# Attention over 3202 keys: the last two keys taken out of the tile loop

## The chip, the cores and the metric

The kernel runs on one core of a Trainium2 chip. The metric is the device time of one execution in microseconds (us): 2633.38 as the median of 3 runs, 2632.97 to 2635.46. All inputs and outputs are float32.

## The reference

One block: a cross attention with a residual, then a mixture of two out of eight experts with a residual. The change touches the attention alone.

```
q = (layernorm(x) @ Wq + bq)     # 4096 x 512, 16 heads of 32
k = (ctx @ Wk + bk)              # 3202 x 512
v = (ctx @ Wv + bv)
A = softmax(q k^T / sqrt(32))    # per head: 4096 queries x 3202 keys
x = x + (A v) @ Wo + bo
x = x + experts(layernorm(x))    # router, top 2 of 8
```

3202 keys are 25 tiles of 128 and two keys over.

## The kernel before

The program has three stages: the projections (about 0 to 292 us), the attention (to about 2142 us), then the output projection, the router and the experts. `attention` (L754) is the stage of interest.

It works in 32 iterations: 4 groups of 4 heads (`NG`), and for each group 8 chunks of 512 queries (`NC`). One iteration runs over `NT` = 26 tiles of 128 keys. The last tile holds `LAST` = 2 keys and is padded: `k_st` is filled to 3328 columns and `v_st` with a zeroed 26th tile.

For a tile, TensorE first makes the scores (`scores`, L1104 to L1130): keys are the stationary operand, 97 rows deep (three rounded parts of 32 rows, and one row that subtracts a shift), and 512 queries stream. The output has keys on partitions. A *pair* is two heads, so it fills two PSUM banks; a tile has two pairs, and `NP` = 52 pairs make an iteration. Three slots of two banks (`S_RING` = 3) hold pairs, so pair n waits until pair n-3 has been exponentiated. ScalarE turns a pair into probabilities with one Exp over 1024 columns (L1020) and writes them to `probs`, a ring of 6 tiles with three more places for the last three tiles. It waits for the earlier user of a place: TensorE's product with the values, and VectorE's addition. TensorE multiplies probabilities with values (`weigh`, L1144, helper `over_keys`, L1137 to L1142): four heads side by side in four column groups of the array, as eight float32 instructions, into bank 6.

The softmax's denominators take a second way. VectorE adds the tiles of probabilities elementwise into `sums[b]` (`add`, L1053 to L1068), 128 x 2048 at a time; two buffers `sums` alternate by iteration. The tiles named in `SUM_ON_PE`, here 13 and 25, are left out there: TensorE multiplies them with `ones` into bank 7. That leaves 24 tiles and 23 additions on VectorE. Early in the next iteration (`SUMS_AT`, behind tile 2's values) `sum_up` multiplies `sums` with `ones` into the same bank and so closes the denominators. ScalarE copies them out (L986, before pair 14), GpSimd's queue spreads them over partitions by DMA, VectorE inverts them (L745, behind addition 9), GpSimd's queue broadcasts the inverses, VectorE multiplies (L751, `normalise`, behind addition 13), ScalarE rounds the result (L992) and GpSimd subtracts for the low part (L867).

The order on each engine is written out by hand. TensorE's is set by `burst_end` (L1132): before it weighs tile t it issues scores up to pair 2t + 7, rounded up so that bursts end where a ring of three slots ends. As 52 is not a multiple of 3, the slots and burst ends shift by one from iteration to iteration and repeat every three.

The keys and values of a group are reloaded in three pieces on SyncE's queue as the previous group's last iteration leaves them (`keys`, `values`). In iteration 0 SyncE also loads `Wo` into `sums[1]` (L949), and ScalarE waits for it before pair 17 and rounds it (L1008).

Of the kernel before, what the change touches and what calls it, by code (L numbers as in the profile page):

```python
# [54 lines left out]
SUM_ON_PE = (13, 25)  # L55
SUMS_AT = 2
SUMS_COPY_AT, INVERT_AT, NORMALISE_AT, SPLIT_AT = 14, 9, 13, 36
# [696 lines left out]
def attention(nc, mem, sb0, sem, psum, unbounded, g):  # L754
# [3 lines left out]
    NP = 2 * NT  # L758
    ROWS = 3 * DH
    FILLS = 3  # L760
# [6 lines left out]
    with mem:  # L767
# [3 lines left out]
        k_st = sb("k_st", [SH + 1, HG, SP_], F32R)  # L771
        q_st = sb("q_st", [SH + 1, 2, HG, CH], F32R)
        v_st = sb("v_st", [P, NT, P], F32)
        ones = sb("ones", [P, DH], F32)
        probs = sb("probs", [P, P_RING + LAG, HG, CH], F32)
# [13 lines left out]
        rows_filled = [sem(f"rows_filled{n}") for n in range(K_PIECES)]  # L789
# [16 lines left out]
        pe_added = sem("pe_added")  # L806
# [18 lines left out]
        def s_slot(phase, n):  # L825


            return (phase * NP + n) % S_RING

# [15 lines left out]
        def fill_rows(eng, heads):  # L845

            for n, (a, m) in enumerate(pieces):
                eng.memset(k_st[SH:SH + 1, heads[0]:heads[1], a * P:min((a + m) * P, S)].bitcast(F32), 1.0).then_inc(rows_filled[n], 1)

        with nc.Block() as block:  # L850
            @block.gpsimd
            def _(pool):
                fill_rows(pool, (0, HG // 2))

                for n in range(K_PIECES):
                    pool.wait_ge(rows_filled[n], 2)
# [12 lines left out]
                def divide(it):  # L869
                    spread_sums(pool, results, it)  # L870
                    broadcast_inverses(pool, results, it)
                    low(it)

                for it in range(NIT - 1):
                    divide(it)

            @block.sync
            def _(sp):
# [21 lines left out]
                def keys(j, before, n):  # L900
                    a, m = pieces[n]
                    if before is not None:

                        sp.wait_ge(s_ready, before * NP + 2 * (a + m))
                    load_k(sp, j, a * P, min((a + m) * P, S) - a * P, k_in[n])

                def values(j, before, n):
                    a, m = pieces[n]
                    if before is not None:

                        sp.wait_ge(pv_done, before * NT + (a + m))
                    full = m - (n == K_PIECES - 1)
                    sp.dma_start(v_st[:, a:a + full, :], v_d[:, a:a + full, ds(j * P, P)]).then_inc(v_in[n], 16)
                    if n == K_PIECES - 1:
                        if before is None:

                            sp.wait_ge(filled, FILLS)
                        sp.dma_start(v_st[0:LAST, NT - 1, :], v_d[0:LAST, NT - 1, ds(j * P, P)]).then_inc(v_in[n], 16)
# [29 lines left out]

                sp.dma_start(wo_raw[:], g["Wo"].rearrange("(j p) n -> p j n", p=P)).then_inc(wo_in, 16)  # L949
# [22 lines left out]
            def _(act):  # L972
# [21 lines left out]
                def step(it, phase):  # L994
                    first = isinstance(it, int) and it == 0
                    for n in range(NP):
# [6 lines left out]
                        t, half = divmod(n, 2)  # L1003
                        slot = s_slot(phase, n)
                        if first and n == NP // 3:

                            act.wait_ge(wo_in, 16)
                            act.activation(wo_hi, wo_raw[:], ACT.Copy).then_inc(wo_hi_ready, 1)  # L1008

                        act.wait_ge(s_ready, it * NP + (n + 1))  # L1010
                        if half == 0:

                            ago, u = before(t)
                            if not (first and ago):
                                act.wait_ge(pv_done, (it + ago) * NT + (u + 1))
                                if u in add_of:
                                    act.wait_ge(added, (it + ago) * adds + add_of[u])
                                if u in SUM_ON_PE:
                                    act.wait_ge(pe_added, (it + ago) * len(SUM_ON_PE) + SUM_ON_PE.index(u) + 1)
# [3 lines left out]
                for it in range(NIT):  # L1023
                    step(it, it % S_RING)
# [3 lines left out]
            def _(dve):  # L1028

                dve.memset(k_st[:, :, S:SP_].bitcast(F32), 0.0).then_inc(filled, 1)  # L1030
                dve.memset(v_st[:, NT - 1, :], 0.0).then_inc(filled, 1)
                dve.memset(ones[:], 1.0).then_inc(filled, 1)
                fill_rows(dve, (HG // 2, HG))
# [21 lines left out]

                def add(it, b, k):
                    t = on_dve[k + 1]

                    dve.wait_ge(exp_done, it * NP + (2 * t + 2))
# [10 lines left out]
                def step(it, b):  # L1070
                    for k in range(adds):
                        add(it, b, k)
# [14 lines left out]
            def _(pe):  # L1087
# [23 lines left out]
                def scores(it, u, i_of, n, first):  # L1111

                    b, (t, half) = u % 2, divmod(n, 2)
# [3 lines left out]
                    if t in piece_of and half == 0:  # L1117

                        pe.wait_ge(k_in[piece_of[t]], (i_of // (NC // 2) + 1) * 48)
                        if first:  # L1120
                            pe.wait_ge(rows_filled[piece_of[t]], 2)
                    slot = s_slot(u % S_RING, n)
# [10 lines left out]
                def burst_end(u, t):  # L1133

                    e = 2 * t + LEAD
                    return e + (S_RING - 1 - e - u) % S_RING
# [7 lines left out]
                def weigh(it, i, t):  # L1144
                    if t in piece_of:

                        n = piece_of[t]
                        pe.wait_ge(v_in[n], (i // (NC // 2) + 1) * (16 * (1 + (n == K_PIECES - 1))))

                    pe.wait_ge(exp_done, it * NP + (2 * t + 2))  # L1150
# [7 lines left out]
                    if t in SUM_ON_PE:  # L1158
                        n = LAST if t == NT - 1 else P
                        if t == SUM_ON_PE[0]:  # L1160

                            pe.wait_ge(sums_copied, it)
                        over_keys(SUM_BANK, lambda h: ones[0:n], lambda h: probs[0:n, p, h, :], t == SUM_ON_PE[0],
                                  False).then_inc(pe_added, 1)
# [8 lines left out]
                def step(it, u, i, i_next):  # L1173

                    first = isinstance(it, int) and it == 0
                    n = 0 if first else burst_end(u - 1, NT - 1) + 1 - NP
                    for t in range(NT):
                        while n <= burst_end(u, t):
# [4 lines left out]
                            n += 1  # L1183
                        weigh(it, i, t)
# [703 lines left out]
```

## Time and profile before

| | |
|---|---|
| median of 3 runs | 2633.38 us |
| the profiled execution's own time | 2634.78 us |
| its span, first to last instruction | 2633.0 us |
| PE busy | 2504.0 us, 95% |
| DVE (VectorE) busy | 2190.0 us, 83% |
| ACT (ScalarE) busy | 1879.6 us, 71% |
| POOL (GpSimd) busy | 487.6 us, 19% |
| granted TensorE clock | 0.971 of full speed, mean |

The shares are means over three stages with different limits. A matmul's end is modelled, so a busy PE isn't a PE at its peak: overlapping matmuls have a duration longer than the distance of their starts, and the distance is what counts. The same holds for a chain of instructions on one engine: the work of an engine is read from starts, not from durations.

### The profile page before, as it was taken

The numbers are of one execution on the slowest core, as the hardware profiler recorded it, in microseconds if no ns is written. First come the engines' busy times: TensorE is split into PE (matmuls) and PEld (weight loads), VectorE is DVE, ScalarE is ACT, GpSimd is POOL, SyncE is SP. The second block draws the span as 40 slices with busy tenths as digits, with TensorE's granted clock in tenths as the row PEclk, the third lists the DMA queues.
The fourth block names the chain that finished last, engine by engine and source line by source line (L and its number), as shares of the span: only waits on it lengthen the run. The fifth ranks groups of instructions, "written<-read, shape, count | busy, mean of one in ns | idle before, by whom it ended". The sixth has DMA issues, their size and how long they took to land. (4 is left out here: it accounts for less than half of the span.)

```text
span 2633.0 us, 38495 instructions
## 1 busy us (share of the span) xinstructions
PE 2504.0 (95%) x14123; PEld 1317.2 (50%) x14123; DVE 2190.0 (83%) x1810; ACT 1879.6 (71%) x2173; POOL 487.6 (19%) x548
## 2 busy tenths in 40 slices
PE   8999489999999999999999999999999988979998
PEld 7878234444434444444444444444444447768776
DVE  4378479999999999999999999999999965666555
ACT  3123379888888888888988889888888855613333
POOL 2123101110000111000011001011000034325664
PEclk9999789999999999999999999999999999969999
DMA  7445861111142111115111111511111038724463
GB/s 260 164 140 208 180 174 26 29 27 31 38 88 63 25 29 33 36 27 113 37 29 33 34 29 25 125 30 33 25 37 25 13 122 297 247 78 135 131 215 124
DMA packets 132882, 231.61 MB, mean 88 GB/s; under 512 B 23634, under 2 KB 56922, under 8 KB 131940
## 3 DMA queue, kind: packets, MB, share of 16 engines
q1 hardware_dynamic: 110468, 177.57, 23.9%
q0 software_dynamic: 22240, 51.68, 6.5%
q8 instruction: 114, 1.87, 0.3%
q14 instruction: 60, 0.49, 0.1%
HBM read 155.32 MB, written 91.66 MB: 94 GB/s over the span
## 5 line engine op out<-in xcount | busy, mean ns | idle before, releaser
L1068 DVE TENSOR_TENSOR sums<-sums,probs 128x2048 f32<-128x2048 f32 x704 | 1644.6, 2336 | 89.9 <-ACT probs L1020 24.7
L1020 ACT ACTIVATE probs<-psum 128x1024 f32<-128x1024 f32 x1664 | 1565.2, 1039 | 207.9 <-PE psum L1129 204.9
L1129 PE MATMUL psum<-q_st,k_st 97*128 97x512 f32 x3328 | 968.6, 421 | 51.7 <-DMA q_st<-shift_scratch 23.1
L1129 PEld LDWEIGHTS psum<-q_st,k_st 97*128 97x128 f32 x3328 | 565.4, 189 | 679.3 <-ACT probs L1020 535.8
L1141 PE MATMUL psum<-probs,v_st 128*32 128x512 f32 x6656 | 835.8, 601 | 0.0
L1141 PEld LDWEIGHTS psum<-probs,v_st 128*32 128x32 f32 x6656 | 158.5, 108 | 370.5 <-issue 300.0
L1836 PE MATMUL psum<-we_hi,wo 128*128 x624 | 219.6, 413 | 8.3 <-issue 5.7
L730 POOL DMA_DIRECT2D sum_scratch<-shared_rows x32 | 18.9, 591 | 989.7 <-ACT shared_rows L986 989.3
L1689 ACT ACTIVATE wo<-psum 128x512 fp32r<-128x512 f32 x78 | 46.5, 597 | 135.6 <-PE psum L1822 112.0
L1836 PEld LDWEIGHTS psum<-we_hi,wo 128*128 128x128 f32 x624 | 119.7, 192 | 35.1 <-issue 9.4
L1836 PE MATMUL psum<-we_lo,wo 128*128 x312 | 124.7, 400 | 0.0
L1682 ACT ACTIVATE shared_rows<-hold 128x512 f32<-128x512 f32 x78 | 63.2, 811 | 65.3 <-DMA hold<-token_rows,near 36.6
L338 POOL TENSOR_TENSOR squares<-o_hi 128x512 fp32r<-128x512 f32 (+1 forms) x60 | 60.6, 1018 | 207.2 <-ACT o_hi L376 120.1
L867 POOL TENSOR_TENSOR shared_rows<-shared_rows 128x512 fp32r<-128x512 f32 x31 | 58.6, 1890 | 217.5 <-ACT shared_rows L992 217.5
L1513 PE MATMUL psum<-wo,att_hi 128*128 128x512 f32 x256 | 85.3, 415 | 7.4 <-DMA att_lo<-ol_scratch 7.4
L1068 DVE TENSOR_TENSOR sums<-probs 128x2048 f32<-128x2048 f32 x32 | 73.2, 2288 | 14.3 <-ACT probs L1020 14.2
L1746 DVE TENSOR_TENSOR res<-psum,be_all 128x512 f32<-128x512 f32 x52 | 36.0, 691 | 56.8 <-PE psum L1836 54.6
L376 ACT ACTIVATE o_hi<-psum,bk_col 128x512 fp32r<-128x512 f32 (+1 forms) x28 | 17.4, 640 | 91.6 <-PE psum L591 91.6
L740 POOL DMA_DIRECT2D shared_rows<-inv_scratch x128 | 63.5, 502 | 49.8 <-DMA inv_scratch<-spread_inv 49.8
L737 POOL DMA_DIRECT2D inv_scratch<-spread_inv x32 | 17.5, 548 | 287.3 <-DVE spread_inv L745 273.9
L1141 PE MATMUL psum<-probs,ones 2*32 2x512 f32 (+1 forms) x512 | 67.3, 596 | 0.0
L1836 PEld LDWEIGHTS psum<-we_lo,wo 128*128 128x128 f32 x312 | 60.2, 193 | 11.2
(197 smaller groups left out, 2036.6 us busy)
## 6 DMA issues: line engine op xcount, KB each, us to landing
q_st<-qh_scratch SPq DMA_DIRECT2D x64, 256.0 KB
token_rows<-rows SPq DMA_DIRECT2D x8, 1040.0 KB, 5.2
xn<-in_x SPq DMA_DIRECT2D x16, 512.0 KB, 6.7
qh_scratch<-o_hi SPq DMA_DIRECT2D x8, 1024.0 KB, 4.5
ql_scratch<-o_lo SPq DMA_DIRECT2D x8, 1024.0 KB, 7.8
q_st<-ql_scratch SPq DMA_DIRECT2D x32, 256.0 KB
token_rows<-in_x SPq DMA_DIRECT2D x1, 8192.0 KB, 33.6
shared_rows<-inv_scratch POOLq DMA_DIRECT2D x128, 64.0 KB, 2.2
```

The source lines that it names most:

```text
L338: pool.tensor_tensor(squares[:, j, 0:w], h, h, ALU.mult).then_inc(squared, 1)
L740: pool.dma_start(a["recip"][h * DH:(h + 1) * DH, :], a["inv_d"][h:h + 1, :].to_broadcast([DH, CH])).then_inc(a["inv_in"], 16)
L867: pool.tensor_tensor(o_low, o_sb, o_high.bitcast(F32), ALU.subtract).then_inc(low_ready, 1)
L1020: nc.scalar.activation(probs[:, p_slot[t], 2 * half:2 * half + 2, :], psum[:, 2 * slot:2 * slot + 2, :], ACT.Exp, scale=SCALE).then_inc(ex ...
L1068: nc.vector.tensor_tensor(sums[b][:], a[:], probs[:, p_slot[t]], ALU.add).then_inc(added, 1)
L1129: mm = nc.tensor.matmul(psum[:, 2 * slot + h % 2, :], k_st[:, h, t * P:(t + 1) * P], q_st[:, b, h, :], start=True, stop=True)
L1141: mm = nc.tensor.matmul(psum[h * DH:(h + 1) * DH, bank, :], lhs(h), rhs(h), start=start, stop=stop)
L1513: mm = pe.matmul(psum[:, i % WO_BANKS, :], A[b][:, j, r, :], W[:, j, :], start=t == 0, stop=t == len(terms) - 1)
L1682: act.activation(xs[s % 2], r[:, 0:D], ACT.Identity, bias=r[:, SHIFT_AT:SHIFT_AT + 1], scale=r[:, RSTD_AT:RSTD_AT + 1]).then_inc(xs_done, 1)
L1689: act.activation(x_hi[s % 2], psum[:, T_BANK + s % 2, :].rearrange("p (k n) -> p k n", k=KT), ACT.Copy).then_inc(xh_done, 1)
L1746: dve.tensor_tensor(res[s % RES][:, 0:D], psum[:, OUT_BANKS[s % 4], :], be_all[:, ds(e, 1), :].rearrange("p o n -> p (o n)"), ALU.add).the ...
L1836: mm = pe.matmul(psum[:, OUT_BANKS[s % 4], :], A[s % 2][:, k, :], W[:, k, ds(e, 1), :].rearrange("p o n -> p (o n)"), start=t == 0, stop=t ...
```

## The change

The tile of two keys goes. `NT` becomes 25 and `NP` 51. The two keys of all four heads, eight rows, become one extra pair, number `REST_PAIR` = 36, that takes one slot of the ring but only its first bank:

- TensorE multiplies, for each of the four heads, a stationary operand of 97 x 72 with the head's queries, and accumulates all four in one bank. Of the 72 rows of output 0 to 7, 32 to 39 and 64 to 71 hold the same eight rows of scores. The operands are columns of `rest_k`, which is zero elsewhere.
- ScalarE takes Exp of 72 x 512 into `rest_probs`; two pairs later it rounds that into `rest_split`.
- VectorE, ahead of addition 19, replaces rows 32 to 39 of `rest_split` by the rounding's remainder.
- TensorE, ahead of tile 22's values, multiplies `rest_v` and `rest_ones` with `rest_split`, into banks 6 and 7, one instruction each (`weigh_rest`).

VectorE copies the two keys' columns of `k_st` to three places of `rest_k` once per group of heads, ahead of addition 9 of its first iteration. `rest_v` is made once, in iteration 0, from twelve small loads on SyncE's queue that come ahead of the load of `Wo`.

`SUM_ON_PE` is tile 12 alone, so VectorE has 24 tiles and 23 additions as before. The places of the steps at the iteration's start move by one tile or one addition. As 51 is a multiple of 3, all iterations have the same slots and burst ends. A ring place whose sum is on PE is released by the next tile's `pv_done` in place of a semaphore of its own.

The diff, cut to its core:

```diff
-SUM_ON_PE = (13, 25)
-SUMS_AT = 2
-SUMS_COPY_AT, INVERT_AT, NORMALISE_AT, SPLIT_AT = 14, 9, 13, 36
+SUM_ON_PE = (12,)
+SUMS_AT = 3
+REST_PAIR = 36
+REST_AT = 22
+REST_KEYS_AT = 9
+REST_LOW_AT = 19
+SUMS_COPY_AT, INVERT_AT, NORMALISE_AT, SPLIT_AT = 16, 10, 14, 38
...
-    NP = 2 * NT
+    NT = NT - 1
+    REST = HG * LAST
+    REST_ROWS = 2 * DH + REST
+    NP = 2 * NT + 1
...
+                sp.wait_ge(filled, FILLS)
+                for o in (0, DH, 2 * DH):
+                    for h in range(HG):
+                        sp.dma_start(rest_raw[o + h * LAST:o + (h + 1) * LAST, :, h * DH:(h + 1) * DH],
+                                     v_d[0:LAST, NT, :].rearrange("p (j x) -> p j x", j=NG)[:, :, h * DH:(h + 1) * DH]).then_inc(wo_in, 16)
                 sp.dma_start(wo_raw[:], g["Wo"].rearrange("(j p) n -> p j n", p=P)).then_inc(wo_in, 16)
...
-                            act.wait_ge(wo_in, 16)
+                            act.wait_ge(wo_in, 16 * (3 * HG + 1))
                             act.activation(wo_hi, wo_raw[:], ACT.Copy).then_inc(wo_hi_ready, 1)
+                            act.wait_ge(rest_v_stage, 3)
+                            act.activation(rest_v[:], rest_raw[:], ACT.Copy).then_inc(rest_v_stage, 1)
+                        if n == REST_PAIR + 2:
+                            act.wait_ge(exp_done, it * NP + (REST_PAIR + 1))
+                            if not first:
+                                act.wait_ge(rest_used, it)
+                            act.activation(rest_split[:], rest_probs[:], ACT.Copy).then_inc(rest_high, 1)
                         act.wait_ge(s_ready, it * NP + (n + 1))
+                        if n == REST_PAIR:
+                            if not first:
+                                act.wait_ge(rest_ready, it)
+                            nc.scalar.activation(rest_probs[:], psum[0:REST_ROWS, 2 * slot, :], ACT.Exp, scale=SCALE).then_inc(exp_done, 1)
+                            continue
...
                     for k in range(adds):
+                        if k == REST_KEYS_AT and it % NC == 0:
+                            dve.wait_ge(filled, FILLS)
+                            dve.wait_ge(k_in[K_PIECES - 1], (it // NC + 1) * 48)
...
+                            for o in (0, DH, 2 * DH):
+                                dve.tensor_copy(rest_places(o), k_st[:, :, S - LAST:S])
+                        if k == REST_LOW_AT:
+                            dve.wait_ge(rest_high, it + 1)
+                            dve.tensor_tensor(rest_split[DH:DH + REST, :], rest_probs[DH:DH + REST, :],
+                                              rest_split[DH:DH + REST, :].bitcast(F32), ALU.subtract).then_inc(rest_ready, 1)
+                        if k == REST_LOW_AT and it == 0:
+                            dve.wait_ge(rest_v_stage, 4)
+                            dve.tensor_tensor(rest_v[2 * DH:], rest_raw[2 * DH:], rest_v[2 * DH:].bitcast(F32), ALU.subtract).then_inc(rest_v_stage, 1)
                         add(it, b, k)
...
+                    if n == REST_PAIR:
+                        if it % NC == 0:
+                            pe.wait_ge(added, it * adds + REST_KEYS_AT + 1)
+                        for h in range(HG):
+                            mm = nc.tensor.matmul(psum[0:REST_ROWS, 2 * slot, :], rest_k[:, h * REST_ROWS:(h + 1) * REST_ROWS],
+                                                  q_st[:, b, h, :], start=h == 0, stop=h == HG - 1)
+                        mm.then_inc(s_ready, 1)
+                        return
...
+                def weigh_rest(it):
+                    pe.wait_ge(rest_ready, it + 1)
+                    if it == 0:
+                        pe.wait_ge(rest_v_stage, 5)
+                    nc.tensor.matmul(psum[:, O_BANK, :], rest_v[:, it // NC, :], rest_split[:], start=False, stop=False)
+                    nc.tensor.matmul(psum[:, SUM_BANK, :], rest_ones[:], rest_split[:], start=False, stop=False).then_inc(rest_used, 1)
...
+                        if t == REST_AT:
+                            weigh_rest(it)
                         weigh(it, i, t)
```

## Rows read from the trace of the kernel before

**Rows 1.** Busy time by stretch: length, then each engine's busy us (instructions), clock, DMA, GB/s.

```profile
382.78:2140.34 1757.56, 1746.43 (x10422) 717.46 (x10421) 1679.30 (x776) 1556.05 (x1702) 173.46 (x248) 1.00 0.17 40
```

**Rows 2.** Timeline, VectorE alone: an iteration's first addition (start us, us, engine, line).

```profile
311.80 2.29 DVE L1068 TENSOR_TENSOR sums<-probs 128x2048 f32<-128x2048 f32 x1 [11.32 <-ACT probs L1020]
...
1007.02 2.29 DVE L1068 TENSOR_TENSOR sums<-probs 128x2048 f32<-128x2048 f32 x1
...
1064.06 2.29 DVE L1068 TENSOR_TENSOR sums<-probs 128x2048 f32<-128x2048 f32 x1 [0.26 <-ACT probs L1020]
...
1120.70 2.28 DVE L1068 TENSOR_TENSOR sums<-probs 128x2048 f32<-128x2048 f32 x1
...
1176.92 2.29 DVE L1068 TENSOR_TENSOR sums<-probs 128x2048 f32<-128x2048 f32 x1
```

**Rows 3.** Timeline of one iteration: VectorE's additions and what stands between them.

```profile
1012.28 19.07 DVE L1068 TENSOR_TENSOR sums<-sums,probs 128x2048 f32<-128x2048 f32 x8 [0.58 <-ACT probs L1020]
...
1031.26 0.24 DVE L745 RECIPROCAL spread_inv<-spread 128x16 f32<-128x16 f32 x1
1031.45 9.48 DVE L1068 TENSOR_TENSOR sums<-sums,probs 128x2048 f32<-128x2048 f32 x4
...
1040.84 0.69 DVE L751 TENSOR_TENSOR shared_rows<-shared_rows 128x512 f32<-128x512 f32 x1
...
1041.45 22.36 DVE L1068 TENSOR_TENSOR sums<-sums,probs 128x2048 f32<-128x2048 f32 x9
...
1042.65 2.23 POOL L867 TENSOR_TENSOR shared_rows<-shared_rows 128x512 fp32r<-128x512 f32 x1 [6.84 <-ACT shared_rows L992]
```

**Rows 4.** The same timeline: TensorE and ScalarE over three tiles, and the extras.

```profile
1029.48 1.65 PE L1129 MATMUL psum<-q_st,k_st 97*128 97x512 f32 x6
1030.25 5.61 ACT L1020 ACTIVATE probs<-psum 128x1024 f32<-128x1024 f32 x6 [0.59 <-PE psum L1129]
...
1031.06 1.06 PE L1141 MATMUL psum<-probs,v_st 128*32 128x512 f32 x8
...
1035.67 1.67 PE L1129 MATMUL psum<-q_st,k_st 97*128 97x512 f32 x6
...
1040.90 1.04 PE L1141 MATMUL psum<-probs,ones 128*32 128x512 f32 x8
...
1041.76 1.04 PE L1141 MATMUL psum<-probs,v_st 128*32 128x512 f32 x8
...
1066.66 1.06 PE L1141 MATMUL psum<-probs,ones 2*32 2x512 f32 x8
1066.79 0.60 ACT L980 ACTIVATE shared_rows<-psum 128x512 f32<-128x512 f32 x1 [0.94 <-PE psum L1141]
...
1067.65 1.06 PE L1141 MATMUL psum<-probs,v_st 128*32 128x512 f32 x8
```

**Rows 5.** Timeline at the attention's start: VectorE's memsets.

```profile
293.46 0.17 DVE L1031 MEMSET v_st<- 128x128 f32 x1
293.59 0.09 DVE L1032 MEMSET ones<- 128x32 f32 x1
293.78 0.27 DVE L848 MEMSET k_st<- 1x256 f32 x1
```

**Rows 6.** Timeline of iteration 0: the load of `Wo` and who waits.

```profile
323.31 0.43 SPq L949 DMA_DIRECT2D sums<-in_Wo  x1
...
338.15 1.91 ACT L1008 ACTIVATE wo<-sums 128x2048 fp32r<-128x2048 f32 x1 [13.44 <-DMA sums<-in_Wo]
...
341.00 5.92 DVE L1068 TENSOR_TENSOR sums<-sums,probs 128x2048 f32<-128x2048 f32 x1 [12.52 <-ACT probs L1020]
```

**Rows 7.** DMA of 292 to 340 us: all packets; an issue, its size, us to landing.

```profile
DMA packets 7810, 10.72 MB, mean 223 GB/s; under 512 B 1067, under 2 KB 4653, under 8 KB 7807
...
sums<-in_Wo SPq DMA_DIRECT2D x1, 1024.0 KB, 14.8
```

**Rows 8.** Timeline at the attention's end.

```profile
2140.40 1.60 PE L1141 MATMUL psum<-sums,ones 128*32 128x512 f32 x8 [1.49 <-DVE sums L1068]
```

More of the change, by code:

```diff
@@ L774, in attention @@
         ones = sb("ones", [P, DH], F32)
+        rest_k = sb("rest_k", [SH + 1, HG * (REST_ROWS + LAST)], F32R)
+        rest_v = sb("rest_v", [REST_ROWS, NG, P], F32R)
+        rest_raw = sb("rest_raw", [REST_ROWS, NG, P], F32)
+        rest_ones = sb("rest_ones", [REST_ROWS, P], F32R)
+        rest_mask = sb("rest_mask", [REST_ROWS, P], F32)
+        rest_probs = sb("rest_probs", [REST_ROWS, CH], F32)
+        rest_split = sb("rest_split", [REST_ROWS, CH], F32R)
         probs = sb("probs", [P, P_RING + LAG, HG, CH], F32)
@@ L788, in attention @@
         filled = sem("filled")
-        rows_filled = [sem(f"rows_filled{n}") for n in range(K_PIECES)]
+        rows_filled = sem("rows_filled")
+        rest_v_stage = sem("rest_v_stage")
+        rest_high = sem("rest_high")
+        rest_ready = sem("rest_ready")
+        rest_used = sem("rest_used")
         ma_k_in = sem("ma_k_in")
@@ L823, in load_q, with place, pair @@
                              src.rearrange("(h d) j l -> d h (j l)", d=DH)[:, :, ds(it * CH, CH)]).then_inc(count, 16)
-        def s_slot(phase, n):
-            return (phase * NP + n) % S_RING
+        assert NP % S_RING == 0 and LAST == 2
+        def place(t, half):
+            n = 2 * t + half
+            return n + (n >= REST_PAIR)
+        def pair(n):
+            return divmod(n - (n > REST_PAIR), 2)
         p_slot = [t % P_RING if t < NT - LAG else P_RING + t - (NT - LAG) for t in range(NT)]
@@ L843, in attention, with piece_end, fill_rows @@
         add_of = {t: max(n, 1) for n, t in enumerate(on_dve)}
-        def fill_rows(eng, heads):
+        def piece_end(n):
+            return S if n == K_PIECES - 1 else sum(pieces[n]) * P
+        def fill_rows(eng, heads, count):
             for n, (a, m) in enumerate(pieces):
-                eng.memset(k_st[SH:SH + 1, heads[0]:heads[1], a * P:min((a + m) * P, S)].bitcast(F32), 1.0).then_inc(rows_filled[n], 1)
+                eng.memset(k_st[SH:SH + 1, heads[0]:heads[1], a * P:piece_end(n)].bitcast(F32), 1.0).then_inc(count, 1)
         with nc.Block() as block:
@@ L852, in _ @@
             def _(pool):
-                fill_rows(pool, (0, HG // 2))
-                for n in range(K_PIECES):
-                    pool.wait_ge(rows_filled[n], 2)
+                fill_rows(pool, (0, HG // 2), rows_filled)
+                pool.wait_ge(rows_filled, K_PIECES)
                 pool.wait_ge(wo_hi_ready, 1)
@@ L911, in values @@
                         sp.wait_ge(pv_done, before * NT + (a + m))
[L912 to L918, printed above, removed]
+                    sp.dma_start(v_st[:, a:a + m, :], v_d[:, a:a + m, ds(j * P, P)]).then_inc(v_in[n], 16)
                 def keys_values(j, before):
@@ L1023, in _ @@
                 for it in range(NIT):
-                    step(it, it % S_RING)
+                    step(it)
                 fetch(NIT - 1)
@@ L1111, in scores @@
                 def scores(it, u, i_of, n, first):
-                    b, (t, half) = u % 2, divmod(n, 2)
+                    b, (t, half) = u % 2, pair(n)
                     if n == 0:
                         pe.wait_ge(q_in[b], (i_of + 1) * 64)
-                    if t in piece_of and half == 0:
+                    if t in piece_of and half == 0 and n != REST_PAIR:
                         pe.wait_ge(k_in[piece_of[t]], (i_of // (NC // 2) + 1) * 48)
                         if first:
-                            pe.wait_ge(rows_filled[piece_of[t]], 2)
-                    slot = s_slot(u % S_RING, n)
+                            pe.wait_ge(rows_filled, piece_of[t] + 1)
+                            pe.wait_ge(filled, FILLS + piece_of[t] + 1)
+                    slot = n % S_RING
                     if n >= S_RING:
@@ L1175, in step @@
                     first = isinstance(it, int) and it == 0
-                    n = 0 if first else burst_end(u - 1, NT - 1) + 1 - NP
+                    n = 0 if first else burst_end(NT - 1) + 1 - NP
                     for t in range(NT):
-                        while n <= burst_end(u, t):
+                        while n <= burst_end(t):
                             if n < NP:
```

53 lines of the change are left out of this document (33 added, 20 removed).

## The prediction

> **What bounds the kernel now.** I first read the busy time by stretch, to get the attention apart from the rest: from iteration 1's first addition to the last addition are 1757.56 us, at full clock, with TensorE busy 1746 us, VectorE 1679 us and ScalarE 1556 us [rows 1]. By shares TensorE would be the limit. So the next view is the timeline, by the distance of starts. It shows two engines near the limit.
>
> VectorE: the distance from one iteration's first addition to the next is 57.04, 56.64 and 56.22 us in turn [rows 2], and this triple repeats with few exceptions; over all 31 it is 1757.56 / 31 = 56.70 us. What VectorE needs, I add up from the rows of one iteration. Eight additions in a row take 19.07 us with seven waits of 0.10 us between them, so one takes (19.07 + 0.10) / 8 = 2.397 us [rows 3]. The reciprocal costs nothing: from 1012.28 to 1031.45 are 19.17 us for eight additions and the reciprocal, and eight additions alone are 19.18. An addition waits for the one before it, and a short instruction fits into that wait. `normalise` costs 0.41: from 1031.45 to 1041.45 are 10.00 us for four additions and it, against 9.59. The last nine additions take 22.36 us where nine are 9 x 2.397 - 0.10 = 21.47: 0.89 more, and GpSimd's subtraction (2.23 us) runs on SBUF just then [rows 3]. An iteration's first addition doesn't wait for its predecessor, which gives back 0.19 (the 0.10 and a start 0.08 ahead of the end, as `normalise` has it). Sum: 23 x 2.397 + 0.41 + 0.89 - 0.19 = 56.24 us. That is the shortest of the three distances, 56.22: in those iterations VectorE has no slack at all. In the others it is late by 0.42 and 0.82 us, in waits for probabilities, one of which is the 0.26 shown [rows 2] and another the 0.58 shown [rows 3].
>
> TensorE and ScalarE work as one loop: a burst of six score products, one tile of values, a burst, two tiles of values. It comes round every 1035.67 - 1029.48 = 6.19 us for three tiles [rows 4], 2.063 us each, and leaves ScalarE 0.59 us idle. For 26 tiles that is 53.6 us. On top come the ones product of the two-key tile (1067.65 - 1066.66 = 0.99), that of tile 13 (1041.76 - 1040.90 = 0.86) and `sum_up` (0.86 likewise): 56.4 us. So this pair of engines needs 56.4 and VectorE 56.2, and the mean of 56.7 is what two nearly equal limits make. A saving on TensorE alone can give back 56.70 - 56.22 = 0.48 us an iteration, 31 x 0.48 = 15 us in all. Everything added on VectorE is paid in full.
>
> **The change part by part.**
>
> *TensorE and ScalarE, per iteration.* One tile goes (2.06) and its ones product (0.99); the tile summed on TensorE stays one, `sum_up` stays. Four products of 97 x 72 with 512 columns come. A burst of six takes 1031.06 - 1029.48 = 1.58 us, 0.26 each [rows 4], so four are 1.05. The two of `weigh_rest` are 0.53 more. Sum: 56.4 - 3.05 + 1.58 = 54.9 us. ScalarE loses two Exps, inside the 2.06, and gains an Exp and a copy of 512 columns, 0.60 each by the copy of the same width [rows 4]. Beside its idle 0.59 of every three tiles they cost from nothing to 1.2 us, so the loop needs 54.9 to 56.1 us.
>
> *VectorE, per iteration.* The additions stay 23, and the reciprocal, `normalise` and GpSimd's subtraction stay, so the 56.22 stay. New is the remainder ahead of addition 19: one subtraction of 512 columns, float32 from SBUF, as `normalise` is; its eight partitions instead of 128 save nothing as far as the duration follows columns. Below, it is bounded by the reciprocal's 0.00 (16 columns) and more nearly by `normalise`'s 0.41; 0.41 is only so small because `normalise` starts 0.08 us before the addition in front of it has ended, and the next addition starts 0.08 before `normalise` ends. The new one reads and writes at partition 32, all its neighbours at partition 0. For such a step there is one row: memsets at partition 0 start 0.04 us ahead of the predecessor's end (293.46 + 0.17 against 293.59), and the one at partition 96 starts 0.10 us behind it (293.59 + 0.09 against 293.78) [rows 5]. With 0.10 on both sides the subtraction costs 0.10 + 0.69 + 0.10 - 0.10 = 0.79 us. I take 0.79, since this row is nearest in what differs, and keep 0.41 for the range. It leaves VectorE at 56.22 + 0.79 = 57.01 us, above the other loop's 56.1: VectorE becomes the only limit, and TensorE's saving is worth nothing beyond the 0.48.
>
> The Trainium skill bears on just this step. "VectorE: DVE Perf Modes", section "Two Vector instructions with no wait between them", says that an instruction which starts in another group of 32 partitions than its predecessor's input or output is held until the predecessor has finished. The memset row agrees; no subtraction in this trace crosses such a border. By the rule the step costs 0.79, and without it 0.41.
>
> *Whether VectorE is really fed.* New waits couple the engines: `weigh_rest`, ahead of tile 22's values, waits for the remainder, and behind it in TensorE's queue are tile 22 and all later scores. At that moment scores of up to the next iteration's third pair are out, so VectorE has tiles 21 to 24 to add, 4 x 2.4 = 9.6 us. TensorE then needs 0.6 for the rest, 1.0 for tile 22 and 0.8 to the first score, ScalarE 1.0: probabilities 3.4 us later. That leaves 6 us. In the other direction the reciprocal and `normalise` keep their distance of four additions, and the spreading of the sums starts two pairs later while VectorE reads it one addition later. In VectorE's queue, behind the waits for `rest_high` and `inv_in`, stand all additions; `rest_high` is made with pair 38, that is tile 18, and read ahead of the addition of tile 21. I count all of that at nothing.
>
> *The sum over iterations 1 to 31.* 31 x 57.01 = 1767.3 against 1757.6: +9.7 us. The ends are set by the last addition in both kernels: TensorE's `sum_up` has been idle for 1.49 us for it [rows 8].
>
> *Copies of the two keys.* Three small copies in four iterations. By the reciprocal's spacing (0.19) three are 0.57, of which 0.19 fit into the addition's wait: 0.4 each time, +1.5 us. Ends: 0 and 3 us. Their wait for the last piece of keys has ten additions, 24 us, since the piece was asked for.
>
> *Iteration 0.* VectorE starves there for 12.52 us because ScalarE waits 13.44 us for `Wo` [rows 6], so what is added before that point is on the path. ScalarE's rounding of `rest_v`: 0.6. The twelve small loads stand ahead of `Wo` in SyncE's queue: at 0.43 us each [rows 6] they put off its issue by 5.2. But `Wo`, 1 MB, lands 14.8 us after its issue, while 223 GB/s are moved [rows 7], which is 4.7 us for 1 MB: some 10 us are backlog, so the later issue mostly shortens the wait in it. I take 1.0, ends 0 and 5.4. VectorE adds the remainder (0.79) and, once, that of `rest_v` at partition 64 (0.79). Together +3.2 us. Memsets, mask and the fills have the 11.32 us in which VectorE waits for its first probabilities [rows 2] as cover. Outside the attention nothing changes.
>
> Total: 9.7 + 1.5 + 3.2 = +14.4 us on the span of 2633.0, on the own time 2634.8 too. That execution is 1.4 us above the median of 2633.4, so I put the difference on the median: **2647.8 us**, 0.55% slower.
>
> **The rivals.**
>
> *The remainder costs 0.41, as `normalise` does.* Then 32 x 0.38 = 12.2 and 0.4 of iteration 0 go: 2635.2 us. For it: the same form and width in the trace. Against it: the partition step of [rows 5], though that is a single row of another operation. The limit stays VectorE, at 56.63.
>
> *The remainder hides and the lateness goes: faster.* If it fitted as the reciprocal does, VectorE would need 56.22, the other loop stays below, and 31 x 0.48 = 14.9 us come back: 2633.4 - 14.9 + 1.5 + 1.6 = 2621.6 us. For it: reciprocal 0.00, and the regular burst pattern. Against it: 0.10 us of wait can't hold 0.69 us of work. It decides from a cost of 0.25 us or less.
>
> *TensorE's stop at tile 22 isn't made good.* If VectorE runs so late that each iteration TensorE's wait adds to its own 54.9 to 56.1 us, the period becomes 57.4 or so: 31 x 0.4 more, 2660 us. For it: additions run slower (2.397) than tiles come (2.063), so VectorE is always late in an iteration's second half. Against it: the 6 us above.
>
> *The twelve loads are paid in full.* 5.4 instead of 1.0: 2652 us. For it: SyncE's issues are spaced 0.43 us or more here. Against it: the backlog.
>
> **How the numbers follow.** Forecast 50% (2643 to 2652), the 0.41 rival 22% (2631 to 2638), the faster one 8%, TensorE's stop 9%, the loads 11%. The range must leave out at most the faster one and the far part of the stop's: 2631 to 2656. A measurement of this kernel tells 0.2%, 5.3 us, from no change, so slower begins at 2638.7: 50 + 9 + 11 = 70%; same is the 0.41 rival, 22%; faster 8%.
>
> **What would show it.** In the changed kernel's timeline the distance of first additions should be 57.0 us in every iteration with no wait for ScalarE; the remainder should start about 0.1 us behind an addition's end, last 0.69 and be followed at 0.1. ScalarE's idle time should now end on VectorE's additions or on TensorE waiting at `weigh_rest`. A period of 56.6 would mean the second case, 56.2 the third. Waits of additions for probabilities in steady iterations would make the whole argument wrong.

## The result: 1.2% slower, twice what was forecast

The changed kernel takes 2663.6 us (median of 4 runs) against 2633.2; ratio 1.0122, 95% interval 1.0097 to 1.0148. The forecast was 2647.8, range 2631 to 2656: right in sign, and 16 us short. The profiled execution's span is 2662.1, 29.1 above that of before.

First the timeline of the changed kernel, VectorE's first addition of an iteration, which answers to [rows 2] (start, duration):

```profile
312.74 2.29 DVE L1124 TENSOR_TENSOR sums<-probs 128x2048 f32<-128x2048 f32 x1 [10.71 <-ACT probs L1062]
...
503.04 2.29 DVE L1124 TENSOR_TENSOR sums<-probs 128x2048 f32<-128x2048 f32 x1
...
562.49 2.29 DVE L1124 TENSOR_TENSOR sums<-probs 128x2048 f32<-128x2048 f32 x1 [1.25 <-ACT probs L1062]
...
619.36 2.28 DVE L1124 TENSOR_TENSOR sums<-probs 128x2048 f32<-128x2048 f32 x1
...
676.22 2.29 DVE L1124 TENSOR_TENSOR sums<-probs 128x2048 f32<-128x2048 f32 x1
...
733.08 2.29 DVE L1124 TENSOR_TENSOR sums<-probs 128x2048 f32<-128x2048 f32 x1
...
794.42 2.29 DVE L1124 TENSOR_TENSOR sums<-probs 128x2048 f32<-128x2048 f32 x1 [4.39 <-ACT probs L1062]
```

Most iterations take 56.87 us without a wait for ScalarE: VectorE is the limit. But some are longer: 59.45 (from 503.04), 61.34 (from 733.08). Iterations are counted from 0, so 7, 15 and 23 are the last of a group; they are the turns of group. Read over all 32, the 29.1 us are:

| | us |
|---|---|
| first addition later (312.74 against 311.80) | 0.9 |
| iteration 0: 75.58 against 70.98 | 4.6 |
| iterations 1 to 31, at 56.87 each, against 1757.56 | 5.4 |
| above 56.87 at two turns of group (iterations 7 and 8, 23 and 24) | 10.9 |
| above 56.87 in iterations 1, 3, 15, 18, 20 | 8.2 |
| behind the last addition | -0.9 |

The 10.9 and the 8.2 were in no term of the forecast, but for up to 0.4 us of copies at a turn. The next rows are one undisturbed iteration of the changed kernel, at the place where ScalarE rounds the last result (compare [rows 3]):

```profile
1058.01 0.68 DVE L755 TENSOR_TENSOR shared_rows<-shared_rows 128x512 f32<-128x512 f32 x1
1058.61 10.37 DVE L1124 TENSOR_TENSOR sums<-sums,probs 128x2048 f32<-128x2048 f32 x4
1058.72 0.63 ACT L1019 ACTIVATE shared_rows<-shared_rows 128x512 fp32r<-128x512 f32 x1 [1.74 <-DVE shared_rows L755]
1059.26 0.61 ACT L1043 ACTIVATE rest_split<-rest_probs 72x512 fp32r<-72x512 f32 x1
...
1059.78 6.46 ACT L1062 ACTIVATE probs<-psum 128x1024 f32<-128x1024 f32 x7
...
1060.83 0.73 PE L1211 MATMUL psum<-q_st,k_st 97*128 97x512 f32 x2 [2.33 <-ACT probs L1062]
...
1069.01 0.68 DVE L1139 TENSOR_TENSOR rest_split<-rest_probs,rest_split 8x512 fp32r<-8x512 f32 x1
1069.72 9.48 DVE L1124 TENSOR_TENSOR sums<-sums,probs 128x2048 f32<-128x2048 f32 x4
```

ScalarE's queue is in order. It waits 1.74 us for VectorE's normalisation, all Exps wait behind it, and TensorE stands still for 2.33 us. Part of that is not the wait: the rounding (0.63) and the copy of the rest (0.61) stand in the same turn of the ring, and in a run below TensorE stops 0.50 us there though ScalarE waits for nothing. In the kernel before nothing waited there; the same rounding starts without idle time in front of it:

```profile
1041.89 0.67 ACT L992 ACTIVATE shared_rows<-shared_rows 128x512 fp32r<-128x512 f32 x1
```

VectorE has a store of tiles, so this stop alone costs nothing: that iteration takes 56.86 us. But now see the busy time by stretch of the changed kernel: the whole attention, the time before, in and behind one of the disturbances, and a turn of group (columns as in [rows 1]; the number behind POOL's is the granted clock):

```profile
388.32:2170.35 1782.03, 1719.64 (x9974) 730.45 (x9970) 1700.02 (x816) 1534.41 (x1701) 194.35 (x248) 0.98 0.17 39
503.04:541.10 38.06, 36.31 (x216) 15.50 (x215) 36.36 (x19) 31.94 (x37) 4.22 (x8) 1.00 0.03 8
541.10:551.30 10.20, 9.33 (x32) 3.14 (x32) 9.82 (x6) 6.41 (x7) 2.07 (x1) 0.50 0.21 53
551.30:562.49 11.19, 11.19 (x66) 5.40 (x66) 8.72 (x5) 9.52 (x11) 0.00 (x0) 1.00 0.31 71
...
786.90:793.70 6.80, 5.47 (x16) 2.70 (x17) 3.03 (x2) 1.36 (x2) 0.00 (x0) 0.50 1.10 221
```

The clock was 1.00 throughout the attention before [rows 1]. Now it falls to half (1.2 of 2.4 GHz) fourteen times, 78.5 us in all. Twelve of the falls begin 38 to 40 us behind an iteration's first addition, where this stop is (1060.83 - 1022.26 = 38.6). What a fall costs follows its length here: at least six of 3.4 us each cost nothing visible, those of 6.8 us in iterations 1, 18 and 20 about 1.0 us each. In iteration 3 it stays down for 10.2 us, VectorE's store runs out, and the iteration takes 2.6 us more. Iteration 15 is the third turn of group, but TensorE did not wait for keys there: it has a fall of 10.2 us like that of iteration 3, and the same 2.6 us.

And at the two other turns of group, TensorE waits for keys:

```profile
777.16 0.81 SPq L835 DMA_DIRECT2D k_st<-kh_scratch  x2
...
788.23 1.22 PE L1211 MATMUL psum<-q_st,k_st 97*128 97x512 f32 x2 [3.93 <-DMA k_st<-kl_scratch]
...
789.49 1.02 ACT L1062 ACTIVATE probs<-psum 128x1024 f32<-128x1024 f32 x1 [3.68 <-PE psum L1211]
```

SyncE asks for the next group's keys only behind the previous result's store, which waits for that same rounding. Counted from the iteration's first addition, this is at 44.1 us (777.16 - 733.08) and was at 42.1 before (764.55 - 722.46), while TensorE, a tile shorter, wants them earlier. The rows of before:

```profile
722.46 2.29 DVE L1068 TENSOR_TENSOR sums<-probs 128x2048 f32<-128x2048 f32 x1 [0.26 <-ACT probs L1020]
...
764.55 2.15 SPq L816 DMA_DIRECT2D k_st<-kh_scratch  x2
```

Behind this wait the clock falls as well (786.90 to 793.70).

### The profile page after: what moved, and what is told of

The parts are those of the page before. It is cut to its first block and busy times, and to the rows that moved or that the text cites. A ratio compares the mean times of both kernels' runs of the same rounds, so it can differ in the third digit from the quotient of the medians.

```text
span 2662.1 us, 37692 instructions
## 1 busy us (share of the span) xinstructions
PE 2484.8 (93%) x13675; PEld 1334.8 (50%) x13675; DVE 2213.9 (83%) x1859; ACT 1859.5 (70%) x2174; POOL 507.3 (19%) x548
## 5 line engine op out<-in xcount | busy, mean ns | idle before, releaser
L1062 ACT ACTIVATE probs<-psum 128x1024 f32<-128x1024 f32 x1600 | 1510.2, 1033 | 200.1 <-PE psum L1211 196.0
L1211 PE MATMUL psum<-q_st,k_st 97*128 97x512 f32 x3200 | 940.2, 426 | 102.8 <-ACT probs L1062 66.6
L1231 PE MATMUL psum<-probs,v_st 128*32 128x512 f32 x6400 | 820.7, 615 | 0.0
L895 POOL TENSOR_TENSOR shared_rows<-shared_rows 128x512 fp32r<-128x512 f32 x31 | 79.5, 2565 | 200.9 <-ACT shared_rows L1019 200.9
L1772 ACT ACTIVATE shared_rows<-hold 128x512 f32<-128x512 f32 x78 | 63.3, 811 | 63.7 <-DMA hold<-token_rows,near 36.4
L418 ACT ACTIVATE o_hi<-psum,bq_col 128x512 fp32r<-128x512 f32 x32 | 22.1, 689 | 56.4 <-PE psum L595 56.4
```

Source lines behind the costliest of these rows:

```text
L1062: nc.scalar.activation(probs[:, p_slot[t], 2 * half:2 * half + 2, :], psum[:, 2 * slot:2 * slot + 2, :], ACT.Exp, scale=SCALE).then_inc(ex ...
L1211: mm = nc.tensor.matmul(psum[:, 2 * slot + h % 2, :], k_st[:, h, t * P:(t + 1) * P], q_st[:, b, h, :], start=True, stop=True)
L1231: mm = nc.tensor.matmul(psum[h * DH:(h + 1) * DH, bank, :], lhs(h), rhs(h), start=start, stop=stop)
L1772: act.activation(xs[s % 2], r[:, 0:D], ACT.Identity, bias=r[:, SHIFT_AT:SHIFT_AT + 1], scale=r[:, RSTD_AT:RSTD_AT + 1]).then_inc(xs_done, 1)
```

## Experiments

Before each kernel's time stands its ratio to the kernel before, timed on the same chip; the absolute level differs between chips (the kernel before took 2632.8 to 2638.1 us).

**The remainder's partition.**

```diff
-   dve.tensor_tensor(rest_split[DH:DH + REST, :], rest_probs[DH:DH + REST, :], rest_split[DH:DH + REST, :] ...
+   dve.tensor_tensor(rest_split[0:REST, :], rest_probs[0:REST, :], rest_split[0:REST, :] ...
```

> The remainder is taken in rows 0 to 7 of rest_split instead of rows 32 to 39, so that the subtraction starts at partition 0 like its neighbours. In the changed kernel it costs 0.64 us (56.87 against 56.22 between first additions of undisturbed iterations). Theory A, the border between groups of partitions holds it on both sides: it costs 0.41 as the normalisation does, undisturbed iterations are 56.63 us, and 31 of them give back 7 us: about 2656. Theory B, the 0.64 is its length whatever the partition: 56.87 and 2663 stay.

Measured: 1.0110 (1.0093 to 1.0127), 2662.0 us. Undisturbed iterations take 56.62 us, so the step costs 0.40 us above 56.22, instead of 0.65. Theory A holds. The rows of this kernel show how:

```profile
998.23 10.36 DVE L1124 TENSOR_TENSOR sums<-sums,probs 128x2048 f32<-128x2048 f32 x4
1008.51 0.67 DVE L1139 TENSOR_TENSOR rest_split<-rest_probs,rest_split 8x512 fp32r<-8x512 f32 x1
1009.11 2.27 DVE L1124 TENSOR_TENSOR sums<-sums,probs 128x2048 f32<-128x2048 f32 x1
```

The remainder starts 0.08 us before the addition has ended (998.23 + 10.36) and the next addition 0.07 before its end; in the changed kernel both start 0.03 behind (1058.61 + 10.37 against 1069.01, and 1069.01 + 0.68 against 1069.72). The rule of the Trainium skill on held instructions ("VectorE: DVE Perf Modes", "Two Vector instructions with no wait between them") agrees with these starts, at 0.25 us for two borders. The total hardly moved: twelve iterations are longer than 57.5 us, six of them by 2.6, and the clock is down for 106 us.

**No remainder.** `rest_ready` is replaced by `rest_high`, and the subtraction goes.

> Leaves out the remainder of the two keys' probabilities (rows 32 to 39 then hold the rounded values a second time, so the two keys are counted twice). VectorE has 0.64 us less per iteration. Theory A (VectorE's work sets the undisturbed period, and its lateness makes ScalarE wait ahead of pair 38, TensorE stop and its clock fall): 56.22 between first additions, the waits for the normalisation shrink by up to 0.64, fewer drops of the clock within the iterations, total 2663 - 20 - some 4 = about 2639. Rival, the drops come from TensorE having less to do and not from that one stop: period 56.22 but as many drops or more, total about 2643 to 2646.

Measured: 1.0050 (1.0033 to 1.0067), 2645.6 us. 56.25 in undisturbed iterations: the need of 56.22 worked out from the rows of before was right. ScalarE's waits for the normalisation shrink too, from 34.6 us to 18.3 in all. Both fit theory A, but the total does not: A said 2639. The rival said 2643 to 2646 with as many falls or more, and there are 15 in iterations 1 to 31, where the changed kernel has 14. The falls inside groups are short (3.4 us, in iterations 0.35 us longer or not at all) but for one; the turns take 61.2, 60.9 and 62.3 us. So this run does not decide between the two. The next one does.

**ScalarE's rounding later.** `SPLIT_AT` 38 becomes 42.

> ScalarE's rounding of the last result moves from ahead of pair 38 to ahead of pair 42, so that it no longer waits for VectorE's normalisation with all Exps behind it. Theory A: the stops of TensorE at that place go, and with them the drops of the granted clock inside the groups (iterations 1, 3, 15, 18, 20 lost 8.2 us together): -8 us. But the result is stored about 3.7 us later, and the next group's keys stand behind that store in SyncE's queue: the three turns of group get longer by up to 3 us each, +5 to +9. Total 2660 to 2665, with another pattern: no drop of the clock except near 787, 1250 and 1710 us. Rival, the drops are TensorE's idle time in general: they stay where they were, total over 2668.

Measured: 1.0106 (1.0089 to 1.0123), 2660.8 us, and the pattern of theory A: iterations inside the groups lose 0.4 us in all where they lost 5.6, and the turns take 61.4, 62.6 and 61.8 (in the changed kernel 61.3, 59.5, 62.7). Around the place of the rounding three falls of 3.4 us are left, where there were twelve falls; the rival had them stay and a total over 2668. Of the 5.2 us given back inside the groups the turns took 2.2. But the edit did not do what it was made for: four pairs later ScalarE still meets VectorE, and waits for the normalisation 22 times, 30.4 us in all (34.6 in the changed kernel). What went is TensorE's stop, whose waits for ScalarE fall from 52.4 us in all to 15.9, the longest 0.85:

```profile
998.19 0.63 ACT L1019 ACTIVATE shared_rows<-shared_rows 128x512 fp32r<-128x512 f32 x1 [1.51 <-DVE shared_rows L755]
...
999.79 0.73 PE L1211 MATMUL psum<-q_st,k_st 97*128 97x512 f32 x2 [0.46 <-ACT probs L1062]
```

TensorE has the values of two tiles to work on during this wait, and the rest's copy stands four pairs away. So the place of the wait in the bursts seems to count, not its length alone.

**The same stop in the kernel before.** `SPLIT_AT` 36 becomes 32; no work is added.

> The kernel before, with ScalarE's rounding of the last result ahead of pair 32 instead of 36, so that there ScalarE has to wait some 2 to 3 us for the normalisation. Theory A: TensorE stops for 1 to 3 us per iteration at that place, the granted clock falls to half for 3 to 10 us in several iterations, and the kernel gets slower by 10 us or more, though no work is added. Rival (the stop is absorbed and the clock doesn't follow so short a stop): within 3 us of 2633, clock 1.0 throughout the attention.

Measured: 1.0642 (1.0624 to 1.0659), 2801.8 us. One constant costs 168 us. Its waits inside the attention, counted to 2140 us; it ends at 2308 (who waited for whom: total, times, longest):

```profile
ACT shared_rows L992 <- DVE shared_rows L751: 104.5, 28, 4.4
PE psum L1129 <- ACT probs L1020: 80.9, 40, 4.1
```

The clock is down for 195 us in the whole attention. Here an iteration is 3 to 7 us longer, far more than in the changed kernel. The likely reason is that TensorE's and ScalarE's loop is itself a limit in this kernel (56.4 of 56.7 us), so a stop is paid, while in the changed kernel it has slack; how the 168 us divide between stop and clock wasn't separated.

**Keys ahead of the store.** Between two groups, SyncE issues the first two pieces of keys and values ahead of the result's store, which is `late()`.

```diff
                     for n in range(K_PIECES):
+                        if n == K_PIECES - 1:
+                            late()
                         keys(j, before, n)
```

> In the last iteration of a group SyncE issues the first two pieces of the next group's keys and values ahead of the previous result's store, not behind it. In the changed kernel TensorE arrives at the next group's second tile 7 us after its keys are asked for and stops 3.9 us; the three turns of group cost 4.9, 2.6 and 6.0 us over an undisturbed period. Theory A (keys stand in SyncE's queue behind a store that waits for ScalarE's rounding): turns at iterations 7 and 23 fall to within 1 us of 56.87, the one at 15, which I put down to the clock, stays or moves; total 2663 - 9 to 12 = 2651 to 2654. Rival (the keys' transfer itself is slow there, whenever it is asked for): no change, 2663.

Measured: 1.0117 (1.0100 to 1.0134), 2667.8 beside 2638.1. The wait for keys is gone and iteration 7 takes 56.86 us: theory A on the queue. The total is a miss. The clock is now down for 109 us, every second iteration from 13 to 23 takes 59.1 to 59.5, and the gain is lost. The turns at 15 and 23 are among these (59.1 and 59.5), without a wait for keys. The stop comes in every iteration, the costly falls in some; what picks these iterations isn't shown.

**Normalisation earlier.** `INVERT_AT` 10 becomes 8, `NORMALISE_AT` 14 becomes 12.

> VectorE inverts behind addition 8 and normalises behind addition 12 (10 and 14 in the changed kernel); ScalarE's rounding stays ahead of pair 38. The normalisation then ends 4.8 us earlier, some 3 us before ScalarE asks for it. Theory A: no stop of TensorE there, no costly drop of the clock inside the groups, -8 us, and the store and the next keys some 1.7 us earlier, -2 to -4: total about 2652 to 2655. Rival (the late place of the rounding was harmless and the drops come from elsewhere): drops and total stay.

Measured: 1.0064 (1.0047 to 1.0081), 2653.8 beside 2638.1: about 15 us of the 30 are gone, a little more than expected. ScalarE still waits up to 1.3 us (16 us in all where it was 33, both counted to 2140 us). Inside the groups 1.1 us are lost where it was 5.6. In the profiled execution the attention ends 14.0 us earlier: 4.5 of it come from inside the groups, 6.2 from the turns, and 3.4 from iteration 0, which the edit hardly touches and which varies by as much between runs (next experiment).

**Small loads behind `Wo`.** The twelve loads come behind it, and ScalarE rounds `rest_v` ahead of pair 36.

> The twelve small loads of the two keys' values come behind the load of Wo on SyncE's queue, and ScalarE rounds rest_v ahead of pair 36 instead of pair 17 of iteration 0. In the changed kernel iteration 0 takes 75.58 us against 70.98, ScalarE waits 12.8 us for Wo and its rounding of rest_v delays the Exps by 0.6. Theory: both leave the path, about 2 to 3 us of the 4.6 go (the remainders' 1.3 us stay): 2660 to 2661. Rival (the extra is TensorE's and VectorE's own work in iteration 0): under 1 us.

Measured: iteration 0 takes 72.3 us where it took 75.6. But it varies: in the six runs with the loads ahead of `Wo` it took 72.2 to 75.6, mean 74.1, and in the five with them behind 71.4 to 74.1, mean 72.3. Two of these five have an addition less on VectorE. So the order is worth about 2 us, no more certain than that. The total was missed: 1.0139 (1.0122 to 1.0156), because eight iterations now take 59 us or more, with the clock down for 116 us.

**All mends in one**: partition, normalisation, keys and small loads.

> All of it in one: remainder at partition 0, normalisation earlier, keys ahead of the store, small loads behind Wo. If the 30 us are understood, every iteration from 1 on takes 56.63 us, the clock costs nothing inside the attention, iteration 0 takes 72 to 73, and the total is about 312.3 + 72.5 + 31 x 56.63 + 491 + 1.9 = 2633: no gain over the kernel before, though TensorE has 1.5 us less to do per iteration, since VectorE has 0.4 more. Over 2640 means that a part isn't understood.

Measured: 1.0018 (1.0008 to 1.0028), 2641.8 beside 2638.1. Iterations take 56.62, the longest 57.0, and the attention's last addition ends at 2141.76 us, against 2140.34 before: 28.6 of the attention's 30.0 us are back (it ended at 2170.35). The clock still falls seven times inside the attention, for 3.4 us each, without a visible cost: none of these iterations is over 56.75. The expected time was level with the kernel before, and this one is 3.7 us above it on the same chip; some 3.5 us of that lie behind the last addition (496.1 against 492.6 us to the end of the profiled executions) and stay unexplained. With one tile on TensorE no gain is left in the attention: VectorE's 56.62 stand against 56.70.

**Two tiles on TensorE**, on top of all mends; the second kernel with `SPLIT_AT` 42.

```diff
-SUM_ON_PE = (12,)
+SUM_ON_PE = (8, 17)
-REST_LOW_AT = 19
+REST_LOW_AT = 18
```

> As the run with all mends, and TensorE sums two tiles (8 and 17) in place of one, so VectorE has 22 additions; the remainder comes ahead of addition 18. VectorE then needs 56.62 - 2.40 = 54.2 us. TensorE's and ScalarE's loop was never the limit in the changed kernel, so its need isn't shown by a period; by the rows of before it is 54.9 to 56.1, plus 0.86 for the second tile: 55.8 to 57.0. If the loop needs about 56.0, iterations take 56.0 and the total is 2633 - 19 = 2614 beside 2633 of before (2618 where before is 2638). Rival, the loop needs 57: no gain, 2645. With little idle time left on TensorE the clock should not fall.

> The same with ScalarE's rounding of the last result ahead of pair 42. With two tiles off VectorE its normalisation is no longer late at pair 38, so theory A expects the same time as the run beside it within 2 us. If it is faster by over 3 us, ScalarE still waited at pair 38 with one addition less in front.

Measured: 0.9930 (0.9916 to 0.9943), 2614.8 beside 2632.8, with 56.01 us per iteration and no fall of the clock: as expected. The second, expected the same, is 0.9873 (0.9858 to 0.9888), **2600.7 us, 1.3% faster than the kernel before**, at 55.49 us. ScalarE did not wait for the normalisation in either, so that reason was wrong. With 38, its rounding stands beside the rest's copy. The rows of the first kernel, then of the second:

```profile
982.69 0.62 ACT L1021 ACTIVATE shared_rows<-shared_rows 128x512 fp32r<-128x512 f32 x1
...
983.11 1.18 PE L1216 MATMUL psum<-q_st,k_st 97*128 97x512 f32 x4
...
983.21 0.62 ACT L1048 ACTIVATE rest_split<-rest_probs 72x512 fp32r<-72x512 f32 x1
...
984.77 7.08 DVE L1129 TENSOR_TENSOR sums<-sums,probs 128x2048 f32<-128x2048 f32 x3 [1.89 <-ACT probs L1067]
...
984.79 0.73 PE L1216 MATMUL psum<-q_st,k_st 97*128 97x512 f32 x2 [0.50 <-ACT probs L1067]
```

```profile
1030.23 0.63 ACT L1048 ACTIVATE rest_split<-rest_probs 72x512 fp32r<-72x512 f32 x1
...
1030.64 1.92 PE L1216 MATMUL psum<-q_st,k_st 97*128 97x512 f32 x6
...
1031.80 7.98 DVE L1129 TENSOR_TENSOR sums<-sums,probs 128x2048 f32<-128x2048 f32 x3 [1.37 <-ACT probs L1067]
...
1034.37 0.65 ACT L1021 ACTIVATE shared_rows<-shared_rows 128x512 fp32r<-128x512 f32 x1
```

Two extra instructions in one turn of the ring stop TensorE for 0.50 us; apart, each is about what ScalarE's idle 0.59 holds. VectorE's wait shrinks by 0.52, and so does the period.

**The stop by itself**, all mends, one tile on TensorE, `SPLIT_AT` 34.

> The run with all mends (one tile on TensorE), with one constant changed: ScalarE's rounding ahead of pair 34, where it has to wait some 4 us for the normalisation. It has the undisturbed 56.62 us otherwise, so it prices the stop and the clock alone. Theory A: TensorE stops some 3 to 4 us per iteration, the granted clock falls in every one or two iterations, and those take 58 to 60 us: +50 to +80 us on 2640. Rival (VectorE has enough tiles in store, and only its own work counts): +5 us or less.

Measured: 1.0023 (1.0011 to 1.0035), 2638.5 beside 2632.8. A clear miss of theory A. The waits of this run, then of the changed kernel, both counted to 2140 us (total, times, longest):

```profile
ACT shared_rows L1021 <- DVE shared_rows L755: 60.0, 28, 3.0
PE psum L1216 <- ACT probs L1067: 29.7, 47, 1.8
```

```profile
ACT shared_rows L1019 <- DVE shared_rows L755: 32.9, 23, 2.0
PE psum L1211 <- ACT probs L1062: 50.0, 30, 2.6
```

ScalarE waits nearly twice as long as in the changed kernel, but TensorE waits for it less, and nowhere the 3 to 4 us expected. So the run does not price a longer stop of TensorE; it shows again that ScalarE's wait isn't passed on in full. The clock is down for 65 us, and three falls of 10.2 us cost about 0.8 us each, not 2.6: a fall has no fixed price either. These start 34 us into the iteration (986.7, with the first addition at 952.8), that of iteration 3 above at 38; earlier in an iteration there seems to be time to refill VectorE's store before the next one's first tiles. That reason is argued, not tested.

**Control: the move to a later place in the kernel before**, `SPLIT_AT` 36 to 40.

> A control: the kernel before with one constant changed, ScalarE's rounding of the last result ahead of pair 40 instead of 36. In the run with two tiles on TensorE the same move was worth 14 us, because there pair 36 and 38 already carry the rest's Exp and copy, and three extra instructions of 0.6 us fell in one turn of ScalarE's ring. Theory: in the kernel before the rounding stands alone, ScalarE's idle 0.59 us per turn covers it, and the move is worth 3 us at most either way: 2630 to 2636. Rival, the late place is worth as much here, so the gain has nothing to do with the change: 2619.

Measured: 1.0068 (1.0050 to 1.0086), 2656.3 beside 2635.6: slower, not same. Inside the groups nothing moved, but the three turns now take 61.1, 61.0 and 63.3 us and the iterations behind two of them 59.1. SyncE asks for the keys behind a store that comes later, as in the changed kernel, here 47.0 us into iteration 7 where it was 42.1:

```profile
770.01 0.81 SPq L816 DMA_DIRECT2D k_st<-kh_scratch  x2
...
780.84 2.08 PE L1129 MATMUL psum<-q_st,k_st 97*128 97x512 f32 x4 [4.49 <-DMA k_st<-kl_scratch]
```

The clock falls three times, for 6.8 us at each turn. I had left this coupling out of the expectation though I knew it by then. It shows the mechanism of the turns on the kernel before, with no other part of the change.

## Why the prediction was right and wrong

- *Two engines near one limit, VectorE needing 56.22 us*: right. Without the remainder the period is 56.25.
- *VectorE becomes the only limit, TensorE's saving is lost*: right in undisturbed iterations.
- *TensorE's and ScalarE's loop at 54.9 to 56.1 us*: a little high. With a second tile (0.86) it should need 55.8 to 57.0, and the second kernel with two tiles runs at 55.49.
- *The remainder at 0.79*: 0.65. The reason, the step between groups of partitions, held: 0.40 without it. The memset row gave 0.10 for a border and it was 0.03. So iterations 1 to 31 gave +5.4 where +9.7 was forecast.
- *The copies, +1.5*: too much. In the runs with all mends the iterations that hold them (8, 16, 24) take 56.75 where others take 56.62, so 0.13 us each.
- *Iteration 0, +3.2*: +4.6 and 0.9 later at its start. `Wo` was asked for 7.5 us later (330.84 against 323.31) and ScalarE rounded it 1.9 later (340.06 against 338.15), 0.9 of that being the later start: the reading of the backlog and its 1.0 us held. (Twelve issues of 0.43 are 5.2 us, as in the sum, not the rival's 5.4.) The loads behind `Wo` gave about 2 back, near my 1.6 for loads and rounding; the rest is within what iteration 0 varies.
- *Whether VectorE is really fed; "I count all of that at nothing"*: this step failed, by some 19 us (the 10.9 and 8.2 of the table). The overestimate of the remainder took 4.3 us off the miss. I asked who feeds VectorE, and listed the queues behind VectorE's and TensorE's new waits. I did not ask who waits for VectorE. As VectorE becomes the limit, the others run ahead of it until they meet it, and they met it at ScalarE's `split`, a wait that was free before and that the change moved in step with `NORMALISE_AT` but not with the lateness. Behind it stood the Exps, TensorE and its clock, and, through the store, the next group's keys. With all mends in one, iterations 1 to 31 take 2.0 us more than 31 undisturbed ones, where they took 19.1 more. How the 19 us divide between stop and clock is not shown, since a mend of one moved the falls elsewhere.
- *TensorE's stop at tile 22* as a rival, 2660 us: its time was nearly right by luck. It had every iteration at about 57.4 us, from a wait of TensorE for the remainder. The changed kernel has no such wait; TensorE's stop came at pair 38 and at the turns.

## What to carry to other kernels

When a change makes another engine the limit, list every wait on that engine, above all those of in-order queues which were free before: each is now met, and what stands behind it is delayed. A wait's cost includes what TensorE's clock does behind a stop. Before judging an idea by its first version, give the freed time to the engine that is the limit: here one tile more on TensorE, with the waits put apart, turned 1.2% slower into 1.3% faster.

## What the runs showed of the hardware

- TensorE's granted clock fell to half in an attention where TensorE was busy 1719.64 of 1782.03 us by the profile and stood still 2.6 us at most inside the groups. Over the runs a fall lasted 3.4 to 13.7 us. With one stop of 0.5 us at most per iteration it didn't fall within the attention (two tiles on TensorE, `SPLIT_AT` 38: 1.00 throughout).
- The cost of a fall was not fixed: 3.4 us down cost 0.4 us at most and mostly nothing, 6.8 us about 1.0 inside the groups of the changed kernel, 10.2 us 2.6 there and 0.8 with `SPLIT_AT` 34.
- Falls that cost time can come in every second iteration (1113.1, 1229.2, 1345.3, 1461.3, 1577.4 us with keys ahead of the store) though the stop is in every one, and an edit elsewhere moves them. Three mends that each worked in their place (partition, keys ahead, loads behind) left the ratio at 1.0110 to 1.0139; the earlier normalisation alone brought it to 1.0064, and all mends together to 1.0018.
